# Third layer's cells: the gather's operands are swapped, and TensorE turns the rows back before the scatter

## The chip, the cores and the metric

The kernel runs on one core of one Trainium2 chip. The metric is the time of one execution in device microseconds. The kernel before took 9364.93 us, the median of 3 runs that lie between 9363.02 and 9368.05 us.

## The reference

A graph of 12,500 nodes with 128 features each and 200,000 edges goes through four layers. Each layer ends in a sum of neighbour rows over the edges and in `x = layernorm(x + layer(x))`. The edges are sorted by destination; the sources are random.

```python
edge_index = jnp.stack([src, dst])
x = _layernorm(x + _L0_gnn_ref(x, src, dst, edge_weight, L0_gnn_W1, L0_gnn_W2))   # two weighted sums
x = _layernorm(x + _L1_gnn_ref(x, ..., src, dst, edge_type_8))                    # typed edges
x = _layernorm(x + _L2_gnn_ref(x, L2_gnn_W, L2_gnn_b, src, dst, edge_weight))     # the layer changed
x = _layernorm(x + _L3_gnn_ref(x, edge_index, ...))                               # attention
```

The change is in the third layer (`_L2_gnn_ref`). Its sum is

```python
h = logmap0(x)
h = h @ W + b
msgs = edge_w[:, None] * h[edge_src]
h = jax.ops.segment_sum(msgs, edge_dst, num_segments=N)
```

## The kernel before, in words

The sum of the third layer is made in `forward_pass` (line 1342), in two ways at once. A part of the edges goes "in order": GpSimd fetches 128 rows at a time from a table in DRAM (line 1394), VectorE builds a matrix that says which row goes to which node with which weight (line 1425), and TensorE multiplies the two (`in_order`, line 1526). The rest of the edges is sorted into cells, and no row of these is fetched on its own.

A cell belongs to a window of 256 source nodes, two source tiles of 128. There are 7 passes `q` over 49 windows, so 343 cells. A cell has 512 slots in 4 blocks of 128 (`FB = 4`). In each block the first 64 slots hold edges whose source lies in tile 0 of the window, the last 64 those with a source in tile 1. One cell takes these steps:

1. SyncE loads the rows of the window from `xparts` (line 1369): each row is split into three bf16 parts whose sum is the fp32 row. It also loads from `srow` (line 1373) the list that says for each slot which source row it wants, to all partitions.
2. VectorE compares the list with the partition number (`to_slots`, line 1409): `reached[r]` is a matrix of zeros and ones, 128 source rows by 512 slots.
3. TensorE gathers (`gather`, line 1504): for each of 4 blocks, 3 parts and 2 tiles it takes the 64 slots' columns of `reached` as the stationary operand and the 128 x 128 rows of the tile's part as the moving one. That is 24 matmuls; the result stands in a PSUM bank with the slots on partitions, 64 of them from each of the two tiles.
4. ScalarE copies the bank to `had[r]` in SBUF as fp32 (`rows_out`, line 1479).
5. VectorE builds `to_dst[r]` (`to_nodes`, line 1417), 4 times 128 slots by 256 nodes, with the edges' weights.
6. TensorE scatters (`scatter`, line 1516): 4 fp32 matmuls with `had` stationary and `to_dst` moving, added into two PSUM banks. The profile shows each fp32 matmul as two records.

TensorE's stream is written out in the order `gather(u + 2)`, `scatter(u)`, and after four of seven cells one `in_order`. So it works two cells ahead. Four sets of buffers `r` go around (line 1353; the cells of a body of seven use the sets 0, 1, 2, 3, 0, 1, 2). Semaphores tie the engines: `xin` and `din` tell of the loads, `reach` of `to_slots`, `gat` of a gather done, `got` of a copy by ScalarE done, `picked` of `to_nodes`, `scat` of a scatter done. A load for a set waits for the gather that last used it (line 1368).

After each pass `q` VectorE adds the two banks to the sums (line 1459), and TensorE clears them (line 1532).

The second layer's `typed_pass` (line 1628) has a gather of its own (line 1822): there the rows' tile is stationary and the slots move, in 6 matmuls.

Of the kernel before, what the change touches and what calls it, by code (L numbers as in the profile page):

```python
# [13 lines left out]
P = 128  # L14
N = 12500
E = 200000
D = 128
# [79 lines left out]
def gnn_kernel(nc, x, src, dst, edge_type_8, edge_weight, W1, W2, Vb, w_comp, root, bias1,  # L97
# [3 lines left out]
    with ctx:  # L101
# [124 lines left out]
        for name in ("load", "copied", "made", "fin", "dve", "pe", "act", "pool", "issued",  # L226
                     "slot", "staged", "g0", "g1", "g2", "g3", "g4", "g5", "g6", "selected", "added",
                     "h1", "h1r", "proj", "projused", "tstored0", "tstored1",
                     "xin0", "xin1", "summed", "rowsT", "var", "sdev", "normed", "stored0", "kept0", "kept1",
                     "xTready", "xTfree", "saved", "tA", "tB",  # L230
                     "onehot", "prod", "packed", "resid", "inrank", "slotted", "weighed", "ranked", "counts", "cntb", "tbuilt",
                     "tsaved", "fcode", "parts", "hi", "rest", "mid", "gat", "scat", "reach", "picked",
                     "got", "sent", "based", "mixed", "scaled", "typed", "rooted", "rootkept", "closed", "natsum", "din0", "din1", "xin2", "xin3", "din2", "din3",
                     "winread", "winT", "targets", "fac", "rowcopy", "selT", "selTc", "atedge", "logit",
                     "ex", "msg", "summedE", "newrow", "newT", "wback",
                     "below", "selb", "vstage", "vT", "bstage", "runmax", "runT", "runlast", "nodemax", "mg"):
            sem(name)
# [1064 lines left out]
        run_base_i = idx[0:1, :, :].rearrange("p a k -> p (a k)")  # L1302

# [38 lines left out]
        def forward_pass(table):  # L1342
# [8 lines left out]
            rowsP = [psum[:, 4 + r, 0:FB * P] for r in range(4)]  # L1351
# [11 lines left out]
            with nc.Block() as block:  # L1363
# [104 lines left out]
                def _(act):  # L1468
# [4 lines left out]

                    def rows_out(q, it, u):
                        n = q * AW + it * FU + u
                        r, before = buffer(u)
                        act.wait_ge(sem("gat"), n + 4)
                        act.wait_ge(sem("scat"), n + (4 - before))
                        nc.scalar.activation(had[r], rowsP[r], ACT.Copy).then_inc(sem("got"), 1)

                    for j in range(3):
                        stage(j, j)
                    rows_out(0, 0, 0)
                    with act.Fori(0, FG) as q:
                        with act.Fori(0, FT7) as it:
                            for u in range(FU):
                                if u in FA:
                                    j = FA.index(u)
                                    stage(q * (FT7 * FM) + it * FM + (j + 3), (j + 3) % FM)
                                rows_out(q, it, u + 1)  # L1490

                @block.tensor
                def _(pe):
                    def gather(q, it, u):
# [4 lines left out]
                        pe.wait_ge(sem("got"), n + (4 - before))  # L1499
                        for i in range(FB):  # L1500
                            for p in range(3):
                                for t in range(2):
                                    at = i * P + t * HS
                                    last = nc.tensor.matmul(rowsP[r][t * HS:(t + 1) * HS, i * P:(i + 1) * P],  # L1504
                                                            reached[r][:, at:at + HS],
                                                            srcwin_x[r][:, t, p, :],
                                                            start=(p == 0), stop=(p == 2))
                        last.then_inc(sem("gat"), 1)
# [34 lines left out]
                    for u in range(2):  # L1543
                        gather(0, 0, u)
                    with pe.Fori(0, FG) as q:
                        pe.wait_ge(sem("sent"), q + 1)
                        clear(True)
                        with pe.Fori(0, FT7) as it:
                            for u in range(FU):
                                gather(q, it, u + 2)  # L1550
                                scatter(q, it, u)
# [1514 lines left out]
```

## Time and profile before

| | |
|---|---|
| median of 3 runs | 9364.93 us |
| span of the profiled execution | 12999.9 us |
| TensorE (PE) busy | 9231.9 us |
| mean granted TensorE clock | 0.787 |
| third layer's `forward_pass`, by its first and last gather | 8120 to 9734 us of the span |

The profile gives of the profiled execution its span alone; no time of its own stands beside it. The span is 3635 us longer than the median of the runs, so the profiled execution is much slower than the timed ones, and a duration in it is not a share of the 9364.93 us. Times of the trace count from the start of the span. PE is TensorE's matmuls, PEld its weight loads, which run beside them. In a timeline row several like instructions are merged: the first number is the start of the first, the second the busy time. The time that a group takes on TensorE is read from the start of its row to the start of the next.

### The profile page before, as it was taken

Reading aid. Unit: us, or ns where it says so; the run is one execution under the profiler, and the core shown is the slowest. Engines: PE = TensorE matmul, PEld = TensorE weight load, DVE = VectorE, ACT = ScalarE, POOL = GpSimd, SP = SyncE. Lnnn points to the kernel's source line nnn. Section 1 sums busy time; section 2 is a strip of 40 time slices with the busy share of each in tenths; the row PEclk is TensorE's granted clock in tenths of the full one; section 3 lists DMA queues with packets and bytes.
Section 4 is the critical chain, followed back from the end, with each engine's and each line's share of the span. In section 5 each row is a group of like instructions: output and inputs, shape, how many; then the busy total and the mean of one; then the engine's idle time right before and its main releaser. Section 6 shows DMA issues by size and latency. Waiting matters only on the chain. (4 is left out here: it accounts for less than half of the span.)

```text
span 12999.9 us, 294862 instructions
## 1 busy us (share of the span) xinstructions
PE 9231.9 (71%) x88712; PEld 7531.3 (58%) x88762; DVE 6869.4 (53%) x25269; ACT 3183.5 (24%) x9441; POOL 5674.7 (44%) x5790
## 2 busy tenths in 40 slices
PE   5977777777777777677777774888873555555555
PEld 5866667776766667634454453666662444444443
DVE  8964444444444444456666665555544555555555
ACT  5841111112111111241111123111113233222223
POOL 3534444442444444305555551444442555555552
PEclk8888888888888888789999996888886555555555
DMA  1013333333333333462222223333332111111113
GB/s 50 28 47 90 91 89 89 88 90 105 90 89 90 89 88 90 95 217 69 67 67 66 67 70 110 101 104 102 101 94 70 39 39 39 39 39 39 39 39 61
DMA packets 962709, 999.47 MB, mean 77 GB/s; under 512 B 141701, under 2 KB 861933, under 8 KB 962093
## 3 DMA queue, kind: packets, MB, share of 16 engines
q1 hardware_dynamic: 774502, 616.47, 17.1%
q0 software_dynamic: 174720, 364.70, 12.9%
q10 hardware_dynamic: 13255, 16.19, 0.4%
q14 instruction: 206, 1.69, 0.0%
q8 instruction: 26, 0.43, 0.0%
HBM read 858.52 MB, written 144.69 MB: 77 GB/s over the span
## 5 line engine op out<-in xcount | busy, mean ns | idle before, releaser
L497 POOL DMA_INDIRECT ring<-att_table,idx x1592 | 1556.3, 978 | 1307.7 <-ACT idx L484 715.5
L1225 PE MATMUL psum<-ring 128*128 128x128 bf16 x21276 | 1547.8, 226 | 784.6 <-issue 766.3
L1225 PEld LDWEIGHTS psum<-ring 128*128 128x128 bf16 x21276 | 1281.3, 101 | 984.9 <-issue 927.9
L1162 DVE TENSOR_SCALAR ring<-sel,iota_col 128x640 bf16<-128x640 bf16 (+1 forms) x1576 | 487.0, 369 | 2368.2 <-remote 1627.6
L1240 PE MATMUL psum<-state 64*128 64x128 f32 x14112 | 1479.8, 356 | 208.9 <-issue 206.7
L1240 PEld LDWEIGHTS psum<-state 64*128 64x128 f32 x14112 | 1318.1, 261 | 345.7 <-issue 330.0
L1148 POOL DMA_INDIRECT ring<-gcn_table,idx x980 | 932.3, 951 | 1300.6 <-ACT idx L1197 996.0
L1679 POOL DMA_INDIRECT state<-rel_table,state x1120 | 1071.1, 956 | 981.8 <-ACT state L1779 657.6
L1148 POOL DMA_INDIRECT ring<-rows,idx x980 | 933.7, 953 | 1289.0 <-ACT idx L1197 993.2
L1169 DVE TENSOR_SCALAR state<-iota_row,state 128x128 f32<-128x128 f32 x5488 | 1457.2, 356 | 0.0
L1394 POOL DMA_INDIRECT state<-hyp_table,state x784 | 755.8, 964 | 855.3 <-ACT state L1471 650.6
L1832 PE MATMUL psum<-weights,state 128*128 128x512 f32 x1576 | 911.5, 663 | 256.2 <-DVE state L1715 192.1
L1209 ACT ACTIVATE state<-psum 128x640 f32<-128x640 f32 (+1 forms) x784 | 476.8, 649 | 2390.3 <-remote 1600.9
L1715 DVE SCALAR_TENSOR_TENSOR state<-psum,state 128x128 f32<-128x128 f32 x2364 | 683.0, 345 | 450.3 <-issue 211.9
L1240 PE MATMUL psum<-state,ring 64*128 64x128 f32 x7840 | 762.1, 319 | 14.6 <-issue 14.5
L1516 PE MATMUL psum<-state 128*128 128x256 f32 x2744 | 767.9, 428 | 0.0
L2939 PE MATMUL psum<-tout 128*128 128x16 bf16 x4728 | 190.3, 173 | 747.2 <-DVE tout L2764 571.8
L1240 PEld LDWEIGHTS psum<-state,ring 64*128 64x128 f32 x7840 | 708.5, 239 | 18.3 <-issue 18.0
L2939 PEld LDWEIGHTS psum<-tout 128*128 128x128 bf16 x4728 | 156.4, 102 | 822.3 <-issue 487.1
L1516 PEld LDWEIGHTS psum<-state 128*128 128x128 f32 x2744 | 547.9, 210 | 108.8 <-issue 8.0
L1504 PE MATMUL psum<-ring,state 128*64 128x128 bf16 x8280 | 397.2, 230 | 272.4 <-issue 270.8
L1840 PEld LDWEIGHTS psum<-state 128*128 128x128 f32 x1568 | 325.1, 207 | 429.4 <-issue 416.4
(447 smaller groups left out, 15814.7 us busy)
## 6 DMA issues: line engine op xcount, KB each, us to landing
ring<-xparts SPq DMA_DIRECT2D x1332, 192.0 KB
ring<-srow SPq DMA_DIRECT2D x544, 128.0 KB
sel<-drow SPq DMA_DIRECT2D x394, 160.0 KB
sel<-drow SPq DMA_DIRECT2D x394, 128.0 KB
rel_table<-tout SPq DMA_DIRECT2D x98, 512.0 KB, 2.6
ring<-att_table,idx POOLq DMA_INDIRECT x1592
ring<-rows SPq DMA_DIRECT2D x56, 448.0 KB
xparts<-state SPq DMA_DIRECT2D x28, 672.0 KB, 3.6
```

What stands on the lines that cost most here:

```text
L497: pool.indirect_dma_start(out=ring[:, u, k, 0:width], out_offset=None, in_=table, in_offset=bass.IndirectOffsetOnAxis(ap=idx[:, u, k:k + 1 ...
L1148: pool.indirect_dma_start(out=fetched[u][:, q, :], out_offset=None, in_=table, in_offset=bass.IndirectOffsetOnAxis(ap=idx[:, u, q:q + 1], ...
L1162: ins = nc.vector.tensor_scalar(reach[u % 2][:, t, :], wanted[u], at[:, :], None, ALU.is_equal)
L1169: ins = nc.vector.tensor_scalar(picks[u][:, j, :], iota_row[:, :], tabS[:, bass.ds(n * SJ + j, 1)], tabW[:, bass.ds(n * SJ + j, 1)], ALU.i ...
L1209: nc.scalar.activation(got[u + v], rowsP[v], ACT.Copy).then_inc(sem("got"), 1)
L1225: last = nc.tensor.matmul(rowsP[v][:, j * P:(j + 1) * P], reach[v][:, t, j * P:(j + 1) * P], xwin[u][:, t, i, :], start=(t + i == 0), stop ...
L1240: last = nc.tensor.matmul(sums[h][:, j * P:(j + 1) * P], rows[h * HS:(h + 1) * HS, :], picks[u][h * HS:(h + 1) * HS, j, :], start=False, s ...
L1394: pool.indirect_dma_start(out=nat_rows[j][:, k, :], out_offset=None, in_=table, in_offset=bass.IndirectOffsetOnAxis(ap=nat_idx[j][:, k:k + ...
L1516: last = nc.tensor.matmul(sums[:, i * SW:(i + 1) * SW], had[r][:, i * P:(i + 1) * P], to_dst[r][:, i, :], start=False, stop=False)
L1679: pool.indirect_dma_start(out=type_rows[j % RB][:, k, :], out_offset=None, in_=table, in_offset=bass.IndirectOffsetOnAxis(ap=type_idx[j % ...
L1715: ins = nc.vector.scalar_tensor_tensor(out=to[:, i, :], in0=by_basis[i][:, b * D:(b + 1) * D], scalar=typeW[b][:, bass.ds(n * FB + i, 1)], ...
L1832: nc.tensor.matmul(by_basis[i], rows_T[R3[u % FU]][:, i * P:(i + 1) * P], V_all, start=True, stop=True).then_inc(sem("proj"), 1)
```

## The change

The gather is turned. The stationary operand is now a tile's part of the rows (source nodes by features), and the slots move, 256 of them at a time: 4 blocks of 64, with a stride of 128. Tile and part give 6 matmuls in place of 24. The result stands with the features on partitions. ScalarE copies it to a new buffer `asked_T[r]` (`turned_out`), TensorE turns each of the 4 blocks with a transpose against the identity back into the same bank (`turn_back`), and ScalarE copies the bank to `had[r]` as before (`rows_out`). The scatter and all other steps are as they were. Two semaphores are new: `turned` and `back`.

```diff
--- before.py
+++ after.py
@@ -231,7 +231,7 @@
...
-                     "winread", "winT", "targets", "fac", "rowcopy", "selT", "selTc", "atedge", "logit",
+                     "turned", "back", "winread", "winT", "targets", "fac", "rowcopy", "selT", "selTc", "atedge", "logit",
...
@@ -1300,6 +1300,8 @@
         nat_sel = [sel_flat[:, i * FK * WIN:(i + 1) * FK * WIN].rearrange("p (k j) -> p k j", j=WIN)
                    for i in range(FM)]
         run_base_i = idx[0:1, :, :].rearrange("p a k -> p (a k)")
+        at = 12 * D + 4 * FB * P // 2
+        asked_T = [ring_flat[:, at + w * FB * P:at + (w + 1) * FB * P] for w in range(3)] + [sq[:, 0:FB * P]]
 
         def forward_setup():
 
@@ -1348,7 +1350,11 @@
             forward_setup()
             sums = psum[:, 0:2, :].rearrange("p b c -> p (b c)")
             nat_bank = [psum[:, 2 + v, 0:WIN] for v in range(2)]
-            rowsP = [psum[:, 4 + r, 0:FB * P] for r in range(4)]
+            bank = [psum[:, 4 + r, 0:FB * P] for r in range(4)]
+
+            def halves(tile, t):
+
+                return tile.rearrange("p (i t s) -> p i t s", t=2, s=HS)[:, :, t, :]
 
             def buffer(u):
 
@@ -1471,15 +1477,23 @@
                         nc.scalar.activation(nat_idx[j], srcT[:, bass.ds(n * FK, FK)], ACT.Copy
                                              ).then_inc(sem("staged"), 1)
 
+                    def turned_out(q, it, u):
+                        n = q * AW + it * FU + u
+                        r, _ = buffer(u)
+                        act.wait_ge(sem("gat"), n + 4)
+                        nc.scalar.activation(asked_T[r], bank[r], ACT.Copy).then_inc(sem("turned"), 1)
+
                     def rows_out(q, it, u):
                         n = q * AW + it * FU + u
                         r, before = buffer(u)
-                        act.wait_ge(sem("gat"), n + 4)
+                        act.wait_ge(sem("back"), n + 1)
                         act.wait_ge(sem("scat"), n + (4 - before))
-                        nc.scalar.activation(had[r], rowsP[r], ACT.Copy).then_inc(sem("got"), 1)
+                        nc.scalar.activation(had[r], bank[r], ACT.Copy).then_inc(sem("got"), 1)
 
                     for j in range(3):
                         stage(j, j)
+                    turned_out(0, 0, 0)
+                    turned_out(0, 0, 1)
                     rows_out(0, 0, 0)
                     with act.Fori(0, FG) as q:
                         with act.Fori(0, FT7) as it:
@@ -1487,6 +1501,7 @@
                                 if u in FA:
                                     j = FA.index(u)
                                     stage(q * (FT7 * FM) + it * FM + (j + 3), (j + 3) % FM)
+                                turned_out(q, it, u + 2)
                                 rows_out(q, it, u + 1)
 
                 @block.tensor
@@ -1497,15 +1512,20 @@
                         pe.wait_ge(sem("reach"), n + 4)
                         pe.wait_ge(sem(f"xin{r}"), loaded(q, it, u))
                         pe.wait_ge(sem("got"), n + (4 - before))
+                        for t in range(2):
+                            for p in range(3):
+                                last = nc.tensor.matmul(halves(bank[r], t), srcwin_x[r][:, t, p, :],
+                                                        halves(reached[r], t), start=(p == 0), stop=(p == 2))
+                        last.then_inc(sem("gat"), 1)
+
+                    def turn_back(q, it, u):
+                        n = q * AW + it * FU + u
+                        r, _ = buffer(u)
+                        pe.wait_ge(sem("turned"), n + 1)
                         for i in range(FB):
-                            for p in range(3):
-                                for t in range(2):
-                                    at = i * P + t * HS
-                                    last = nc.tensor.matmul(rowsP[r][t * HS:(t + 1) * HS, i * P:(i + 1) * P],
-                                                            reached[r][:, at:at + HS],
-                                                            srcwin_x[r][:, t, p, :],
-                                                            start=(p == 0), stop=(p == 2))
-                        last.then_inc(sem("gat"), 1)
+                            last = nc.tensor.transpose(bank[r][:, i * P:(i + 1) * P],
+                                                       asked_T[r][:, i * P:(i + 1) * P], ident[:, :])
+                        last.then_inc(sem("back"), 1)
 
                     def scatter(q, it, u):
                         n = q * AW + it * FU + u
@@ -1542,12 +1562,14 @@
                                      start=True, stop=True).then_inc(sem("natsum"), 1)
                     for u in range(2):
                         gather(0, 0, u)
+                    turn_back(0, 0, 0)
                     with pe.Fori(0, FG) as q:
                         pe.wait_ge(sem("sent"), q + 1)
                         clear(True)
                         with pe.Fori(0, FT7) as it:
                             for u in range(FU):
                                 gather(q, it, u + 2)
+                                turn_back(q, it, u + 1)
                                 scatter(q, it, u)
                                 if u in FA:
                                     j = FA.index(u)
```

TensorE's queue, in the body of the loop over `it`, from the gather of one cell to the in-order matmuls: lines 1504, 1516 and 1526 are `gather`, `scatter` and `in_order`. Before, of the gather of cell 3 and the scatter of cell 1:

```order
L1498 ISA [waits reach]
L1504 MATMUL psum<-ring,state 64x128 [waits got,xin3]
L1504 MATMUL psum<-ring,state 64x128 x23
L1513 REGISTER_ALU
L1514 REGISTER_ALU [waits got]
L1516 MATMUL psum<-state 128x256 [waits picked]
L1516 MATMUL psum<-state 128x256 x3
```

Now (1517 is the gather, 1526 the turning back, 1536 the scatter):

```order
L1513 ISA [waits reach]
L1517 MATMUL psum<-state,ring 128x4x64 [waits got,xin3]
L1517 MATMUL psum<-state,ring 128x4x64 x5
L1526 MATMUL psum<-ident,ring 128x128 [waits turned]
L1526 MATMUL psum<-ident,ring 128x128 x3
L1533 REGISTER_ALU
L1536 MATMUL psum<-state 128x256 [waits picked,got]
L1536 MATMUL psum<-state 128x256 x3
```

Between the gather of a cell and the scatter of the cell two before it stands the turning back of the cell between, with a wait for `turned`. The scatter's 4 matmuls have the same place behind it.

ScalarE's queue in the same body: 1471 is `stage` (the indices for GpSimd), 1479 is `rows_out`. Before:

```order
L1477 REGISTER_ALU
L1478 REGISTER_ALU [waits gat]
L1479 ACTIVATE state<-psum 128x512 [waits scat]
L1477 REGISTER_ALU
L1479 ACTIVATE state<-psum 128x512 [waits scat,gat]
L1470 REGISTER_ALU
L1471 ISA [waits natsum]
L1471 ACTIVATE state<-srcT 128x4
```

Now (1477 is `stage`, 1484 is `turned_out`, 1491 is `rows_out`):

```order
L1483 REGISTER_ALU
L1484 ACTIVATE sq<-psum 128x512 [waits gat]
L1489 REGISTER_ALU
L1491 ACTIVATE state<-psum 128x512 [waits scat,back]
L1483 REGISTER_ALU
L1484 ACTIVATE ring<-psum 128x512 [waits gat]
L1489 REGISTER_ALU
L1491 ACTIVATE state<-psum 128x512 [waits scat,back]
L1476 REGISTER_ALU
L1477 ISA [waits natsum]
L1477 ACTIVATE state<-srcT 128x4
```

Each cell has two copies of 512 columns in place of one. The first waits for the gather of the cell that stands two ahead, the second for the turning back.

## Rows read from the trace of the kernel before

**Rows 1.** The page: span, TensorE's busy time, its granted clock in 40 slices.
```profile
span 12999.9 us, 294862 instructions
PE 9231.9 (71%) x88712; PEld 7531.3 (58%) x88762; DVE 6869.4 (53%) x25269; ACT 3183.5 (24%) x9441; POOL 5674.7 (44%) x5790
...
PEclk8888888888888888789999996888886555555555
```

**Rows 2.** Groups of instructions, 8120 to 9740 us (count, busy us, mean ns, idle before):
```profile
L1394 POOL DMA_INDIRECT state<-hyp_table,state x782 | 753.9, 964 | 841.3 <-ACT state L1471 636.9 <-issue 204.4
L1516 PEld LDWEIGHTS psum<-state 128*128 128x128 f32 x2744 | 547.9, 210 | 108.8 <-issue 8.0 <-ACT state L1479 0.7
L1417 DVE TENSOR_SCALAR state<-tout,state 128x256 f32<-128x256 f32 x1372 | 479.2, 413 | 0.9 <-issue 0.6
...
L1504 PEld LDWEIGHTS psum<-ring,state 128*64 128x64 bf16 x8280 | 286.1, 114 | 404.1 <-issue 375.0 <-DVE state L1409 4.8
...
L1425 DVE TENSOR_SCALAR sel<-iota_row,dstrel,wT 128x128 f32<-128x128 f32 x784 | 221.2, 353 | 0.3 <-issue 0.3
...
L1479 ACT ACTIVATE state<-psum 128x512 f32<-128x512 f32 x344 | 202.5, 597 | 803.3 <-remote 662.1 <-PE psum L1504 118.8 <-issue 21.6
L1409 DVE TENSOR_SCALAR state<-ring,iota_col 128x512 bf16<-128x512 bf16 x345 | 124.0, 359 | 656.4 <-DMA ring<-srow 623.4 <-issue 28.4 <-PE psum L1504 3.5
```

**Rows 3.** Timeline of TensorE in the third layer (start us, busy us):
```profile
8602.44 0.86 PE L1504 MATMUL psum<-ring,state 128*64 128x128 bf16 x24
8603.24 1.99 PE L1516 MATMUL psum<-state 128*128 128x256 f32 x8
8605.16 0.86 PE L1504 MATMUL psum<-ring,state 128*64 128x128 bf16 x24
8605.95 1.99 PE L1516 MATMUL psum<-state 128*128 128x256 f32 x8
8607.78 1.05 PE L1526 MATMUL psum<-sel,state 128*128 128x128 f32 x8
8608.76 0.41 PE L1504 MATMUL psum<-ring,state 128*64 128x128 bf16 x8
```

**Rows 4.** The same timeline, where single matmuls stand apart:
```profile
8563.58 0.23 PE L1504 MATMUL psum<-ring,state 128*64 128x128 bf16 x1 [0.45 <-issue]
8565.00 0.23 PE L1504 MATMUL psum<-ring,state 128*64 128x128 bf16 x1 [1.18 <-issue]
8565.72 0.22 PE L1504 MATMUL psum<-ring,state 128*64 128x128 bf16 x1 [0.50 <-issue]
...
8567.85 0.76 PE L1504 MATMUL psum<-ring,state 128*64 128x128 bf16 x20 [0.50 <-issue]
```

**Rows 5.** Timeline of TensorE in the second layer's typed pass:
```profile
6209.02 0.82 PE L1822 MATMUL psum<-ring 128*128 128x256 bf16 x6
6209.67 1.02 PE L1832 MATMUL psum<-weights,state 128*128 128x512 f32 x2
6210.53 0.59 PE L1840 MATMUL psum<-state 128*128 128x256 f32 x2
6210.97 1.02 PE L1832 MATMUL psum<-weights,state 128*128 128x512 f32 x2
...
6212.26 1.05 PE L1852 MATMUL psum<-sel,state 128*128 128x128 f32 x8
6213.15 0.59 PE L1832 MATMUL psum<-weights,state 128*128 128x512 f32 x1
```

**Rows 6.** Timeline of TensorE, seven fp32 transposes in the projection:
```profile
5573.84 0.93 PE L2264 MATMUL psum<-ident,ring 128*128 128x128 f32 x7
```

**Rows 7.** Timeline of TensorE, seven fp32 transposes ahead of the third layer:
```profile
7899.64 1.76 PE L2105 MATMUL psum<-ident,ring 128*128 128x128 f32 x7 [2.55 <-ACT ring L2068]
```

**Rows 8.** Timeline of ScalarE beside rows 3, the copy after the first gather:
```profile
8603.42 0.60 ACT L1479 ACTIVATE state<-psum 128x512 f32<-128x512 f32 x1 [0.56 <-PE psum L1504]
```

**Rows 9.** Busy us and count of each engine, granted clock, DMA share in one stretch:
```profile
8500.00:9000.00 500.00, 408.01 (x3929) 329.65 (x3934) 257.80 (x851) 72.52 (x169) 235.69 (x244) 0.88 0.37 103
```

## The prediction

> **What bounds the kernel now.** I read the page first. TensorE is busy for 9231.9 of the span's 12999.9 us [rows 1]. The timed runs take 9364.93 us, 3635 us less than the span, and TensorE idles in the span for 12999.9 - 9231.9 = 3768 us. So nearly all of TensorE's idle time in the profile would have to be missing from the timed runs. That decides how the rest is read: what TensorE has to stream is real, what it stands still for in this profile mostly is not. One reservation: the mean granted clock is 0.787, and matmuls that ran at the lower level would be shorter in a run with fewer stops, so a part of the idle time could survive.
>
> Next the groups of the third layer's cells, 8120 to 9740 us, some 1615 us between first and last gather, for 343 cells: 4.7 us a cell. The reader is to see which engine lacks slack [rows 2]. ScalarE is busy for 202.5 us with its copies, VectorE for 479.2 + 221.2 + 124.0 us with its large groups. GpSimd is a different matter: its rows are 0.96 us each, and 4 of them serve one in-order step. TensorE has the most to do. Its weight loads for the gather waited 375.0 us for nothing that the profile shows, 4.8 us for VectorE and, before the scatter, 0.7 us for ScalarE. VectorE waited 623.4 us for the lists from DRAM, but TensorE nearly never waited for VectorE, so these loads arrive early enough.
>
> The 375.0 us have a shape [rows 4]: single matmuls of one gather start 0.7 or 1.4 us apart, and then 20 run at full rate. A gather outside such a stop takes the same time again and again. The timeline without stops gives the floor of TensorE [rows 3], from start to start:
> - gather 8605.95 - 8605.16 = 0.79 us
> - scatter 8605.16 - 8603.24 = 1.92 us if a gather follows, 8607.78 - 8605.95 = 1.83 us if the in-order step follows
> - in-order step 8608.76 - 8607.78 = 0.98 us
>
> A body of seven cells with four in-order steps takes 3 x (0.79 + 1.92) + 4 x (0.79 + 1.83 + 0.98) = 22.5 us, 3.22 us a cell, 1104 us for 49 bodies. The granted clock was 0.88 in 500 us of this stage, stops included [rows 9]; the rows of the floor are at its upper level, 2.4 GHz. GpSimd needs 16 x 0.964 + 204.4 / 49 = 19.6 us in a body, fetches and the "issue" gaps between them [rows 2]: near, but shorter than 22.5. VectorE's three groups are (479.2 + 221.2 + 124.0) / 49 = 16.8 us. I take it that in the timed runs TensorE bounds this stage.
>
> **The gather.** 24 matmuls with 64 stationary columns go, 6 with 128 stationary and 256 moving columns come. The trace has this form, in the second layer [rows 5]: 6209.67 - 6209.02 = 0.65 us for six, in the same strided reading of the slots. Against 0.79 us that is -0.14 us a cell.
>
> The old form costs its neighbours too. The same 8 in-order records take 6213.15 - 6212.26 = 0.89 us in the second layer, and 0.98 us before the gather of 64 columns. The scatter is 1.92 us before that gather and 1.83 before another step. So -0.09 us a cell where TensorE enters the form. The 8 records of the scatter should take less still: two records of that shape take 6210.97 - 6210.53 = 0.44 us in the second layer, and two of twice the width 6210.53 - 6209.67 = 0.86 us, so 8 take 1.72 to 1.76 us and not 1.83. I take 1.73. I read the missing 0.10 us as the first weight load, which the narrow gather ahead of it holds up. This is the least certain gain. Together -0.33 us a cell with it, -0.23 without.
>
> A rule speaks against this. The Trainium skill, TensorEngine Tiling (Array Packing), section Theoretical Speedup, gives two matmuls with at most 64 stationary columns up to twice the throughput, as they run side by side in halves of the array. By it 24 matmuls of 128 moving columns stream as long as 12, and 12 x 128 is 6 x 256: the turn would gain nothing in the gather. The section Key Properties adds that a change of tiling mode drains the engine. The trace bears out both: 0.79 against 0.65 us is a small gain for a quarter of the matmuls, and the 0.09 us at the border look like the drain. By the first rule alone the sum below would be 343 x 0.44 = 151 us.
>
> **The turning back.** 4 fp32 transposes of 128 x 128 come to each cell. Seven of them took 0.93 us with a last one of 0.27 us [rows 6], so (0.93 - 0.27) / 6 = 0.11 us each: +0.44 us. At the lower clock seven took 1.76 us [rows 7], 0.22 us each. I take 0.11, since the neighbours here are dense.
>
> **Sum.** New cell: 0.65 + 0.44 + 1.73 = 2.82 us, with the in-order step 3.71. Old: 2.71 and 3.60 (2.72 and 3.61 as the trace repeats them). That is +0.11 us a cell, 343 x 0.11 = +38 us. Bounds: without the gain at the scatter +0.21 us, +72 us; with transposes that stream as the pairs of the old gather do, 0.79 / 12 = 0.07 us each, -0.05 us a cell, -17 us; with all transposes at the lower clock, +0.55 us, +189 us. I take +40 us, from the rows at the upper clock, and 9364.93 + 40 = 9405 us. In the profile's own terms the span would go to 13,040 us if the stops stayed.
>
> **What is hidden.** ScalarE's added copy is 0.60 us [rows 8], 343 x 0.60 = 206 us of work on an engine with 1.2 us of 3.3 us used. It costs nothing while it comes in time. After a gather ends (8603.30) the copy starts at 8603.42. So `turned` of cell n + 2 is there some 0.7 us after its gather, and TensorE asks for it one step later, 3 us on. Behind `turned_out` of n + 2 on ScalarE stands `rows_out` of n + 1, which also waits for the turning back of n + 1. It starts at about 0.65 + 0.12 + 0.60 = 1.4 us after the gather began, ends at 2.0, and the scatter of n + 1 asks for it at 2.8 + 1.1 = 3.9 us. Slack 1.9 us. The bank of a set is free one step later than before, and its next gather comes a step after that. `stage` now stands behind a later copy, by up to 2 us, and each fetch is ordered a whole body ahead. The loads wait for `gat` as before; SyncE's and GpSimd's queues keep their order. If the cover were gone, the wait would be one copy a cell, 206 us.
>
> **Rivals.**
> 1. Faster: the stops are real, at least in part. They stand at the gathers of narrow matmuls [rows 4] and the code that causes them shrinks: a body has 7 x 64 + 64 = 512 matmul and load records before and 7 x 36 + 64 = 316 after, 38% fewer. If the 375.0 us were in the timed runs and scaled with the count, 0.38 x 375 = 143 us would go: 9365 + 40 - 143 = 9262 us; with half of the stops 9333 us. It decides from the point where more than 105 us of the 375 (40 / 0.38) exist in a timed run. For it: the stops are always at L1504 here. Against: 3635 us must be missing from the profile's time.
> 2. No change: loads or GpSimd pace the stage at 3.3 us a cell or more, and the added work fills TensorE's waits: 9365 to 9380 us. For it: VectorE's 623.4 us of waiting for lists. Against: the 4.8 us of TensorE.
> 3. Slower: ScalarE's chain ends last. A wait of 0.3 us a cell adds 103 us: 9508 us. Against: the slack of 1.9 us.
> 4. Slower: TensorE falls to its lower level more often, since the transposes carry less load. If the clock fell in one cell of ten, 0.1 x 343 x 3.4 = 117 us: 9522 us. For it: rows 7. Against: rows 6 are at the upper level without a dense neighbour.
>
> The Trainium skill, TensorE: Matmul & The Clock Gate, section Part 4: PE-mode transpose, has it that transposes do not count as work for the clock gate. It would make rival 4 likelier; rows 6 neither prove nor refute it, since other work ran before.
>
> **How the numbers follow.** What a measurement of this kernel can tell from no change is about 0.2%, 19 us. Forecast (+19 to +80 us): 0.56. Rivals 3 and 4, or any cost over +80: 0.10. Between -19 and +19: 0.16, rival 2 and the low bound of the sum. Rival 1: 0.18. So faster 0.18, same 0.16, slower 0.66. The range leaves out a half of rival 1 and most of rivals 3 and 4: 9330 to 9465 us. The likeliest case's own range is 9384 to 9445.
>
> **What would show it.** Six gather matmuls start to start in 0.65 us; four transposes in 0.44 us; eight scatter records in 1.73 us (1.83 would put +72 in place of +38); the in-order step in 0.89 us. No wait of TensorE for ScalarE at the turning back or the scatter above a few us. A granted clock of 0.85 or more in the stage. The forecast is wrong if a body without stops is shorter than 22.5 us, if TensorE's stops shrink and the timed runs follow, or if a body is bound at GpSimd's 19.6 us.

## The result and the profile after

| | before | after |
|---|---|---|
| median of 5 runs | 9364.93 us | 9400.06 us |
| lowest, highest | 9363.02, 9375.23 us | 9390.7, 9409.83 us |
| ratio, 95% interval | | 1.0036, [1.0023, 1.0048] |
| predicted | | 9405 us (9330 to 9465) |

The changed kernel is slower by 35 us, between 22 and 45 us by the interval. Forecast were 40 us.

The page of the changed kernel, with span and busy time:

```profile
span 9388.9 us, 285834 instructions
PE 7707.4 (82%) x83928; PEld 6594.8 (70%) x83928; DVE 6867.2 (73%) x25269; ACT 3450.3 (37%) x9786; POOL 5726.0 (61%) x5790
```

Its span is 9388.9 us, as long as a timed run. The span of [rows 1] was 12999.9 us. The two profiles can't be compared stage by stage before it is known what made the first one long; the first experiment is about that.

TensorE's timeline in the third layer's cells (start us, busy us; 1517 is the gather, 1526 the turning back, 1536 the scatter, 1546 the in-order step):

```profile
6204.44 0.82 PE L1517 MATMUL psum<-state,ring 128*128 128x256 bf16 x6
6205.10 0.60 PE L1526 MATMUL psum<-ident,ring 128*128 128x128 f32 x4
6205.53 1.89 PE L1536 MATMUL psum<-state 128*128 128x256 f32 x8
6207.26 1.05 PE L1546 MATMUL psum<-sel,state 128*128 128x128 f32 x8
6208.15 0.82 PE L1517 MATMUL psum<-state,ring 128*128 128x256 bf16 x6
```

From start to start: gather 0.66 us, turning back 0.43, scatter 1.73, in-order step 0.89. These rows answer to [rows 3], where a gather took 0.79, a scatter 1.83 to 1.92 and the in-order step 0.98 us. A cell with an in-order step is 6208.15 - 6204.44 = 3.71 us.

Busy us, count, granted clock, DMA share and GB/s of 500 us of the stage, which answers to [rows 9]:

```profile
5800.00:6300.00 500.00, 482.33 (x3218) 433.08 (x3217) 342.96 (x1129) 164.42 (x366) 309.85 (x326) 0.98 0.51 135
```

TensorE is busy for 482.33 of 500 us at a granted clock of 0.98, so nearly all of this stretch runs at the upper of the two levels, 2.4 GHz, although four transposes stand in each cell. GpSimd's 309.85 us and VectorE's 342.96 us leave both slack.

Groups of the stage (count, busy us, mean ns, idle before), which answer to [rows 2]:

```profile
L1517 PEld LDWEIGHTS psum<-state,ring 128*128 128x128 bf16 x2070 | 204.6, 99 | 54.4 <-issue 9.5 <-DVE state L1415 4.1
L1491 ACT ACTIVATE state<-psum 128x512 f32<-128x512 f32 x344 | 203.5, 592 | 1.8 <-PE psum L1526 1.8
```

TensorE's weight loads for the gather waited 9.5 us for nothing that shows and 4.1 us for VectorE. No line of the whole list has TensorE waiting for ScalarE. ScalarE's copies of one cell in the timeline (1484 is `turned_out`, 1491 `rows_out`):

```profile
6205.30 0.60 ACT L1484 ACTIVATE ring<-psum 128x512 f32<-128x512 f32 x1 [1.64 <-PE psum L1517]
...
6205.79 0.59 ACT L1491 ACTIVATE state<-psum 128x512 f32<-128x512 f32 x1
```

They follow each other without a gap. The second ends at 6205.79 + 0.59 = 6206.38, 1.94 us after the gather began, and the scatter that wants it begins one step later, after 6208.15.

### The profile page after: what moved, and what is told of

Same layout as the page of the kernel before. It is cut to its first block and busy times, and to the rows that moved or that the text cites. A ratio compares the mean times of both kernels' runs of the same rounds, so it can differ in the third digit from the quotient of the medians.

```text
span 9388.9 us, 285834 instructions
## 1 busy us (share of the span) xinstructions
PE 7707.4 (82%) x83928; PEld 6594.8 (70%) x83928; DVE 6867.2 (73%) x25269; ACT 3450.3 (37%) x9786; POOL 5726.0 (61%) x5790
## 5 line engine op out<-in xcount | busy, mean ns | idle before, releaser
L1225 PE MATMUL psum<-ring 128*128 128x128 bf16 x21276 | 1271.4, 221 | 54.6 <-DVE ring L1162 54.6
L1240 PE MATMUL psum<-state 64*128 64x128 f32 x14112 | 958.7, 278 | 0.0
L1240 PEld LDWEIGHTS psum<-state 64*128 64x128 f32 x14112 | 850.7, 188 | 44.4 <-issue 4.8
L1854 PE MATMUL psum<-weights,state 128*128 128x512 f32 x1576 | 815.2, 599 | 42.8 <-DVE state L1737 42.8
L1536 PE MATMUL psum<-state 128*128 128x256 f32 x2744 | 652.8, 381 | 0.0
L1815 ACT ACTIVATE state<-psum,state 128x128 f32<-128x128 f32 x788 | 289.9, 368 | 810.5 <-PE psum L1854 809.7
L1240 PE MATMUL psum<-state,ring 64*128 64x128 f32 x7840 | 568.7, 272 | 0.0
L1197 ACT ACTIVATE idx<-state 128x3 int32 (+2 forms) x788 | 160.7, 204 | 1032.8 <-PE psum L1240 923.8
L1240 PEld LDWEIGHTS psum<-state,ring 64*128 64x128 f32 x7840 | 502.8, 188 | 0.0
L1423 DVE TENSOR_SCALAR state<-tout,state 128x256 f32<-128x256 f32 x1372 | 474.8, 407 | 0.0
```

The source lines that it names most:

```text
L1225: last = nc.tensor.matmul(rowsP[v][:, j * P:(j + 1) * P], reach[v][:, t, j * P:(j + 1) * P], xwin[u][:, t, i, :], start=(t + i == 0), stop ...
L1240: last = nc.tensor.matmul(sums[h][:, j * P:(j + 1) * P], rows[h * HS:(h + 1) * HS, :], picks[u][h * HS:(h + 1) * HS, j, :], start=False, s ...
L1536: last = nc.tensor.matmul(sums[:, i * SW:(i + 1) * SW], had[r][:, i * P:(i + 1) * P], to_dst[r][:, i, :], start=False, stop=False)
L1854: nc.tensor.matmul(by_basis[i], rows_T[R3[u % FU]][:, i * P:(i + 1) * P], V_all, start=True, stop=True).then_inc(sem("proj"), 1)
```

## The experiments

Theory A is the prediction's: TensorE's stream bounds the stage, and each change counts by its start-to-start times. All times are medians; the kernels ran in three batches, and each batch ran the kernel before as well (9353.72, 9359.21 and 9358.05 us). A difference is against the kernel before of the same batch.

### The kernel before, profiled again

No edit.

> The kernel before, unchanged, profiled once more. Theory A (TensorE's stream bounds the stage, and the stops of the first profile are not part of a timed run): the span comes near 9365 us, the third layer's cells take about 1165 us, a body of seven 22.5 us, and the gather's "issue" idle time falls from 375 us to under 20. Theory B (the stops belong to the narrow matmuls): the stage takes about 1615 us again, with a stop in nearly every body.

Measured: one run of 9343.64 us. Its page, the weight loads of its gather in the stage, and TensorE's timeline:

```profile
span 9341.8 us, 294912 instructions
PE 7739.6 (83%) x88762; PEld 6557.2 (70%) x88762; DVE 6851.6 (73%) x25269; ACT 3293.7 (35%) x9441; POOL 5716.6 (61%) x5790
```

```profile
L1504 PEld LDWEIGHTS psum<-ring,state 128*64 128x64 bf16 x8280 | 246.7, 111 | 85.9 <-issue 57.9 <-DVE state L1409 4.2 <-ACT state L1479 0.8
```

```profile
6202.11 0.86 PE L1504 MATMUL psum<-ring,state 128*64 128x128 bf16 x24
6202.90 1.99 PE L1516 MATMUL psum<-state 128*128 128x256 f32 x8
6204.73 1.05 PE L1526 MATMUL psum<-sel,state 128*128 128x128 f32 x8
6205.72 0.86 PE L1504 MATMUL psum<-ring,state 128*64 128x128 bf16 x24
```

The span is 9341.8 us. The "issue" idle time before the gather's weight loads, 375.0 us in [rows 2], is 57.9 us, more than the 20 us I expected; the full-width gather of the changed kernel has 9.5, so most of it seems to come with the entry into the narrow form. No matmul stands apart as in [rows 4]. The durations are those of [rows 3]: 0.79, 1.83 and 0.99 us. So the stops belonged to that one profiled execution, and Theory B falls. They did not belong to narrow matmuls even there: the first layer's gather (line 1225), whose matmuls have 128 stationary columns, was stretched as well, from 2735 us in the new profile to 4592 us in the first, with 1694.3 us of "issue" idle time in 2444 places against 42.7 us in 13. The new row comes first:

```profile
L1225 PE MATMUL psum<-ring x21276: 219/219/314, 868.1 to 3603.4; 128*128 128x128 bf16 x199
```

```profile
L1225 PE MATMUL psum<-ring x21276: 216/219/314, 873.8 to 5465.9; 128*128 128x128 bf16 x199
```

In 500 us of the third layer's stage the kernel before has the granted clock of the changed one, 0.98, where [rows 9] had 0.88 with the stops:

```profile
5800.00:6300.00 500.00, 482.45 (x5350) 405.24 (x5349) 348.59 (x1165) 102.62 (x228) 319.99 (x335) 0.98 0.52 139
```

With this profile the stage can be compared; the rows give times of single records and the start of the first and last scatter, of the kernel before and of the changed one:

```profile
L1516 PE MATMUL psum<-state x2744: 379/379/796, 5735.0 to 6896.7; 128*128 128x256 f32 x196
```

```profile
L1536 PE MATMUL psum<-state x2744: 379/379/635, 5735.2 to 6930.0; 128*128 128x256 f32 x196
```

6896.7 - 5735.0 = 1161.7 us against 6930.0 - 5735.2 = 1194.8 us: +33 us, nearly the whole of the 35 us. The two spans differ by 47 us; the other 14 us lie behind the stage, where the kernels are alike, and are not the change's.

### The turned gather without the turning back

```diff
-                        act.wait_ge(sem("back"), n + 1)
+                        act.wait_ge(sem("gat"), n + 4)
...
-                                turned_out(q, it, u + 2)
...
-                                turn_back(q, it, u + 1)
```

> The turned gather alone: ScalarE's added copy and the four transposes are left out, so the scatter gets rows that are not turned back. Theory A: per cell 0.65 + 1.73 us in place of 0.79 + 1.92, and 0.89 in place of 0.98 for the in-order step: -0.33 us x 343 = -113 us against before, 9252 us. Theory C (array packing alone: 12 x 128 columns are 6 x 256, nothing is gained): no change, 9365 us. Theory D (the stage is paced by loads or GpSimd): no change either, but with waits of TensorE in the profile.

Measured: 9236.52 us, ratio 0.9873 [0.9856, 0.9889] to before, which is -117 us against 9353.72. Theory A said -113. TensorE's timeline (1514 gather, 1533 scatter, 1543 in-order step):

```profile
6208.62 0.82 PE L1514 MATMUL psum<-state,ring 128*128 128x256 bf16 x6
6209.27 1.89 PE L1533 MATMUL psum<-state 128*128 128x256 f32 x8
6211.00 1.05 PE L1543 MATMUL psum<-sel,state 128*128 128x128 f32 x8
6211.89 0.82 PE L1514 MATMUL psum<-state,ring 128*128 128x256 bf16 x6
```

The gather takes 0.65 us, the scatter 1.73 and the in-order step 0.89. Theories C and D said no change: both fall for this kernel. The turned gather alone is a real gain.

### The old gather with the turning back

In the changed kernel:

```diff
-                        for t in range(2):
+                        for i in range(FB):
                             for p in range(3):
-                                last = nc.tensor.matmul(halves(bank[r], t), srcwin_x[r][:, t, p, :],
-                                                        halves(reached[r], t), start=(p == 0), stop=(p == 2))
+                                for t in range(2):
+                                    at = i * P + t * HS
+                                    last = nc.tensor.matmul(bank[r][t * HS:(t + 1) * HS, i * P:(i + 1) * P],
+                                                            reached[r][:, at:at + HS],
+                                                            srcwin_x[r][:, t, p, :],
+                                                            start=(p == 0), stop=(p == 2))
```

> The old gather of 24 narrow matmuls, with ScalarE's added copy and the four transposes behind it, so the scatter gets the rows turned once too often. Theory A: the transposes cost 4 x 0.11 = 0.44 us a cell, but they also stand between the narrow gather and the scatter and take over its late first weight load, so +0.40 to +0.44 us: +137 to +150 us against before, 9502 to 9515 us. Theory D (paced elsewhere): under +60 us.

Measured: 9491.7 us, ratio 1.0149 [1.0132, 1.0166], +138 us. TensorE's timeline (1519 gather, 1530 turning back, 1540 scatter):

```profile
6204.27 0.66 PE L1530 MATMUL psum<-ident,sq 128*128 128x128 f32 x4
6204.77 1.89 PE L1540 MATMUL psum<-state 128*128 128x256 f32 x8
6206.59 0.86 PE L1519 MATMUL psum<-ring,state 128*64 128x128 bf16 x24
```

The scatter takes 1.82 us before a gather, where it took 1.92 in [rows 3]: the late first weight load has gone to the transposes, which take 6204.77 - 6204.27 = 0.50 us here and 0.43 in the changed kernel (medians over the stage 0.49 and 0.44). So the narrow gather does delay what stands behind it, whatever that is; that it does so through the first weight load is read from the start times and not shown apart. Per cell 0.50 - 0.10 = 0.40 us, 137 us by 343 cells, and 138 are measured. The two halves give -117 + 138 = +21 us, and together they are +35. The late load explains the rest: the first half saves all its 0.10 us, the second turns it into 0.06 us at the transposes and saves 0.04 us, but the change can save it only once. 0.04 x 343 = 14 us have to be added to the 21. This is read from the rows; each of the two ratios is uncertain by some 16 us, so the times alone do not show these 14 us.

### ScalarE's added copy alone

The old gather stands in the changed kernel, as in the section before; `turn_back` is left out, and `rows_out` waits for `turned` in place of `back`. So ScalarE copies each bank twice, and nobody reads the first copy.

> The kernel before with ScalarE's added copy of each bank and without transposes: `rows_out` copies the bank a second time, behind a copy that nobody reads. Theory A (the added copy is hidden): no change, within 10 us of before. Theory F (a part of the change's +0.4% is ScalarE's second copy): slower by the same share, up to 0.60 us x 343 = 206 us if it lay open.

Measured: 9360.37 us, ratio 1.0 [0.9991, 1.0009]. 343 copies of 0.60 us on ScalarE cost nothing that can be measured (8 us at most by the interval). Theory F falls.

### One part of the rows in place of three

```diff
-                            for p in range(3):
+                            for p in range(1):
...
```

> The kernel before with one of the three bf16 parts of the rows gathered and two left out: 8 narrow matmuls a cell in place of 24. Theory A (fixed cost of 0.28 us a cell at the borders of the narrow form, plus 0.056 us for each pair): 8 pairs fewer, -0.45 us x 343 = -154 us, and in the profile the in-order step stays 0.98 us, the scatter 1.92 and 1.83 us. Theory G (the border cost is a tail of the 24 matmuls and shrinks with them): those three shrink too, up to -0.28 us x 2/3 x 343 = -64 us more, -218 us. Where TensorE comes below 19.6 us a body GpSimd could take over: TensorE's body would be 22.6 - 3.1 = 19.5 us, so a part of the 154 us may not come.

Measured: 9211.83 us, ratio 0.9844 [0.983, 0.9857], -147 us. TensorE's timeline:

```profile
6204.87 1.05 PE L1526 MATMUL psum<-sel,state 128*128 128x128 f32 x8
6205.85 0.41 PE L1504 MATMUL psum<-ring,state 128*64 128x128 bf16 x8
6206.20 2.00 PE L1516 MATMUL psum<-state 128*128 128x256 f32 x8
6208.12 0.41 PE L1504 MATMUL psum<-ring,state 128*64 128x128 bf16 x8
```

The in-order step before the gather is 6205.85 - 6204.87 = 0.98 us and the scatter before a gather 6208.12 - 6206.20 = 1.92 us, as with 24 matmuls. The gather is 0.35 us. Over all cells the medians are 0.791 and 0.344 us, so the 8 pairs that go took 0.056 us each; 4 pairs are 0.224 us, and 0.12 us of the gather is fixed. Theory G falls: the cost at the borders is the same for 8 and for 24 matmuls. It is 0.12 + 0.09 + 0.10 us a cell, 0.316 before rounding, a little more than the 0.28 that I had put down.

### The turning back without cover

```diff
-                                turn_back(q, it, u + 1)
+                                turn_back(q, it, u + 2)
```

(and in the prologue the turning back behind each of the two gathers)

> The changed kernel with the turning back directly behind the gather of the same cell, so that nothing covers ScalarE's first copy. Theory A: TensorE waits for the gather's tail, the copy of 0.60 us and the signals, about 0.95 us a cell less the little that stays hidden: 343 x 0.85 to 0.95 = +290 to +325 us against the changed kernel, near 9700 us. Rival: the 64-deep queue of work behind it hides a part and it is under +150 us.

Measured: 9721.52 us, ratio 1.0388 [1.0374, 1.0402] to before: +362 us, and +321 against the changed kernel's 9400. TensorE's timeline:

```profile
6205.90 0.82 PE L1517 MATMUL psum<-state,ring 128*128 128x256 bf16 x6
6207.41 0.66 PE L1526 MATMUL psum<-ident,ring 128*128 128x128 f32 x4 [0.69 <-ACT ring L1484]
6207.90 1.89 PE L1536 MATMUL psum<-state 128*128 128x256 f32 x8
```

The turning back now starts 1.51 us after the gather in place of 0.66: +0.85 us, and its own time is 0.49 in place of 0.43 us, 0.91 x 343 = 312 us. This is what the order of the changed kernel, one cell between gather and turning back, is worth. The transposes' 0.49 us are those of the run with the old gather, though no narrow gather stands here: a start behind a wait costs them the same.

### Fewer borders: gathers in groups

If the borders of the narrow form cost 0.3 us a cell, the kernel before can shed them without any turning. In its body on TensorE, with groups of four and three:

```diff
-                            for u in range(FU):
-                                gather(q, it, u + 2)
-                                scatter(q, it, u)
-                                if u in FA:
+                            for group in ((0, 1, 2, 3), (4, 5, 6)):
+                                for u in group:
+                                    gather(q, it, u + 2)
+                                for u in group:
+                                    scatter(q, it, u)
+                                    if u in FA:
...
```

> The kernel before with another order on TensorE: in each body of seven cells the gathers stand in two groups, four and three, with their scatters and in-order steps behind them. Same matmuls. Theory A (each entry into the narrow form costs 0.09 us and each exit 0.19 us): 5 of 7 entries and exits go, 5 x 0.28 x 49 = 69 us, 9296 us. Theory E (the old gather is dear in itself and its borders cost nothing): no change. If the tighter order makes TensorE wait for VectorE or ScalarE at a group's start, slower.

Measured: 9488.98 us, ratio 1.0141 [1.0124, 1.0158], +135 us where I had expected -69. TensorE's timeline and VectorE's over the same time (1409 `to_slots`, 1417 `to_nodes`, 1435 `add_before`):

```profile
6201.38 0.86 PE L1504 MATMUL psum<-ring,state 128*64 128x128 bf16 x24 [1.88 <-DVE state L1409]
6203.34 0.86 PE L1504 MATMUL psum<-ring,state 128*64 128x128 bf16 x24 [1.10 <-DVE state L1409]
```

```profile
6200.57 0.27 DVE L1435 TENSOR_TENSOR acc<-acc,psum 128x128 f32 x1
6200.77 0.34 DVE L1409 TENSOR_SCALAR state<-ring,iota_col 128x512 bf16<-128x512 bf16 x1
6201.03 1.38 DVE L1417 TENSOR_SCALAR state<-tout,state 128x256 f32<-128x256 f32 x4
6202.83 0.39 DVE L1409 TENSOR_SCALAR state<-ring,iota_col 128x512 bf16<-128x512 bf16 x1 [0.41 <-DMA ring<-srow]
...
6208.89 0.29 DVE L1435 TENSOR_TENSOR acc<-acc,psum 128x128 f32 x1 [3.25 <-PE psum L1526]
```

The gathers at 6201.38 and 6203.34 each start 0.5 to 0.6 us after the VectorE comparison at 6200.77 and 6202.83. The first of these comparisons stands in VectorE's queue behind `to_nodes` of a cell and behind `add_before`, and the `add_before` at 6208.89 waited 3.25 us for an in-order step on TensorE, which now stands later. The second, for the fourth gather of the group, waited for its list from DRAM. In the kernel text the load for a cell waits for the gather three cells before it (line 1368 waits for `gat` at `n + 1`, and `gat` starts at 3), and of a fourth cell that is the first gather of its own group. So TensorE's order had been changed without that of its partners, VectorE and SyncE.

> The kernel before with TensorE's gathers in groups of two, two, two and one, and nothing else moved. The groups of four failed because VectorE's comparison for the third and fourth gather stood behind its waits for in-order steps. Theory A: with pairs each comparison is ready, 3 of 7 entries and exits of the narrow form go, 3 x 0.28 x 49 = -41 us against before. Theory H (any group makes TensorE wait for VectorE): no change or slower, with waits at L1504 for L1409.

The edit is the same with groups of two, two, two and one. Measured: 9313.23 us, ratio 0.9948 [0.9935, 0.9962], -46 us, where -41 were expected. TensorE's timeline:

```profile
6202.11 1.53 PE L1504 MATMUL psum<-ring,state 128*64 128x128 bf16 x48
6203.57 3.72 PE L1516 MATMUL psum<-state 128*128 128x256 f32 x16
6207.13 1.05 PE L1526 MATMUL psum<-sel,state 128*128 128x128 f32 x8
6208.11 1.53 PE L1504 MATMUL psum<-ring,state 128*64 128x128 bf16 x48
```

Two gathers take 6203.57 - 6202.11 = 1.46 us, not 1.58, and the two scatters behind them 6207.13 - 6203.57 = 3.56 us, not 1.92 + 1.83 = 3.75. None of these gathers waits. The first and last scatter of the stage:

```profile
L1516 PE MATMUL psum<-state x2744: 379/379/796, 5750.1 to 6864.5; 128*128 128x256 f32 x196
```

6864.5 - 5750.1 = 1114.4 us against 1161.7: -47 us, and 3 borders x 0.316 us x 49 bodies are 46. Theory H falls.

> The changed kernel with its turned gathers in groups of two, two, two and one, as the kernel before had them in the run that was 46 us faster. Theory A (the borders that grouping takes away are those of the narrow form, 0.12 + 0.09 + 0.10 us each): the turned gather has no such border, so no change against the changed kernel, 9395 to 9405 us. Theory I (grouping helps by itself, through fewer waits or a steadier stream): 30 us or more faster than the changed kernel.

The same pairs in the changed kernel, with each turning back ahead of its scatter. Measured: 9399.7 us, ratio 1.0045 [1.0032, 1.0059] to before, +42 us where the changed kernel had +35, its own time within the intervals. So pairs save nothing where no narrow gather stands: what they save in the kernel before is the narrow form's border. Theory I falls.

> The kernel before with TensorE's gathers in groups of three, two and two. Theory A: 4 of 7 borders of the narrow form go, 4 x 0.316 x 49 = -62 us against before, if VectorE's comparison for the third gather is there in time; where it is not, waits at L1504 for L1409 eat it, up to 2 us a body, 98 us.

Groups of three, two and two. Measured: 9415.2 us, ratio 1.006 [1.0046, 1.0074], +57 us. TensorE's timeline:

```profile
6218.81 1.53 PE L1504 MATMUL psum<-ring,state 128*64 128x128 bf16 x48
6222.18 0.86 PE L1504 MATMUL psum<-ring,state 128*64 128x128 bf16 x24 [1.84 <-DVE state L1409]
```

The third gather of the group of three starts 3.37 us after the first two and waits 1.84 us for VectorE. The saving of 62 us is more than eaten.

The last regrouping has groups of four and three on TensorE and the same groups on VectorE:

```diff
-                            for u in range(FU):
-                                to_slots(q, it, u + 2)
-                                to_nodes(q, it, u)
+                            for group in ((0, 1, 2, 3), (4, 5, 6)):
+                                for u in group:
+                                    to_slots(q, it, u + 2)
+                                for u in group:
+                                    to_nodes(q, it, u)
...
```

> Groups of four and three, as in the run that was 135 us slower, but with VectorE's comparisons for a group also standing together, ahead of its other work for the group. Theory A: if the waits for VectorE go, 5 of 7 borders go, 5 x 0.316 x 49 = -77 us against before. If VectorE's in-order steps still stand between the groups, the waits at the head of the second group stay, up to 2 us a body, and it is near or above before.

Measured: 9568.69 us, ratio 1.0222 [1.0208, 1.0236], +211 us. One group of four in the timeline (1373 the load of a list, 1409 `to_slots`, 1506 gather, 1518 scatter, 1528 in-order step; other rows are left out):

```profile
6198.43 2.20 PE L1506 MATMUL psum<-ring,state 128*64 128x128 bf16 x72
6200.05 0.35 SPq L1373 DMA_DIRECT2D ring<-srow  x1
6203.48 0.35 DVE L1409 TENSOR_SCALAR state<-ring,iota_col 128x512 bf16<-128x512 bf16 x1 [5.74 <-DMA ring<-srow]
6203.96 1.49 PE L1506 MATMUL psum<-ring,state 128*64 128x128 bf16 x24 [3.33 <-DVE state L1409]
6205.39 5.85 PE L1518 MATMUL psum<-state 128*128 128x256 f32 x16
6211.08 1.05 PE L1528 MATMUL psum<-sel,state 128*128 128x128 f32 x8
```

Three gathers run without a wait. The list for the fourth is ordered only at 6200.05, after the first of them is done, and the comparison comes 3.43 us later; VectorE waited 5.74 us for it, and TensorE 3.33 us for the comparison. This is the load's wait again, which VectorE's new order does not touch. The stop has a second price: TensorE's clock falls. Busy us, count, granted clock, DMA share of the 4 us behind the stop:

```profile
6204.00:6208.00 4.00, 4.00 (x30) 3.37 (x31) 4.00 (x14) 0.00 (x0) 2.19 (x3) 0.50 0.67 199
```

At a granted clock of 0.50, the lower level, the fourth gather takes 1.43 us in place of 0.79, and the two scatters 5.69 us in place of 3.56. From 5800 to 6300 us the granted clock is 0.88 here, 0.96 in the runs with groups of four on TensorE alone and of three, and 0.98 in those with pairs and without groups. TensorE's waits for the comparison are much the same with VectorE's old order and its new one (158 and 164 us), so it is in the clock that the last 76 us, from +135 to +211, were for the most part lost: the two scatters between gathers and in-order step alone take 54 us more in all, 8 us of it in waits for `to_nodes`. An earlier load of the lists and another order of `add_before` were not tried. Pairs are the best version that makes the whole sum, 46 us below before and 87 us below the changed kernel's 9400.

## Why the prediction was right

**What bounds the stage.** That the stops are not in a timed run was the point on which all rested, and the second profile of the kernel before bears it out: 9341.8 us, gathers without stops. Rival 1, the stops, had 0.18 and is refuted. But the step that led there was in part luck. It set the 3768 us in which TensorE was idle beside the 3635 us of difference, as if nearly all idle time had to go. In the second profile TensorE is still idle for 9341.8 - 7739.6 = 1602 us, and its busy time is 1492 us shorter; the prediction's reservation about the lower clock points that way, but it puts no size to it. That the two numbers stood so close was chance. [rows 3], gathers at the upper clock without stops, were the sound part of the argument. That GpSimd's 19.6 us a body does not bind holds at 22.6 and at 23.3 us. In the run with one part TensorE's body is 19.4 us by its start-to-start times, and 7 of the expected 154 us were missing. GpSimd was not seen to take them: of the cells' matmuls the gather waited 8.5 us and the scatter 3.1 us for VectorE (7.0 and none in the kernel before), and the in-order step, which uses GpSimd's rows, for nothing.

**The gather.** -0.14 us by the second layer's rows; measured 0.79 to 0.66. The second layer's kernel text has the same form, and its duration carried over.

**The neighbours.** -0.09 at the entry and -0.10 at the scatter: measured 0.98 to 0.89, and 1.83 to 1.73. The second was "the least certain gain", and it decided between +38 and +72 us. The run with the old gather and the turning back shows it apart from the rest, and the single-part run shows that it does not shrink with the number of matmuls. How the hardware makes it is inferred from start times alone.

**The packed matmuls.** By the Trainium skill, TensorEngine Tiling (Array Packing), section Theoretical Speedup, alone the turn would gain nothing and the sum would be +151 us. The streams agree with it (12 narrow pairs at 0.056 us against 6 matmuls at 0.11). The Trainium skill has in the section Key Properties of that page that a change of tiling mode drains the engine; the runs agree, with a cost of 0.32 us a cell that does not depend on the number of matmuls, but none shows that a drain makes it. The gain of the turned gather is the border that it avoids, not its stream: 12 x 0.056 = 0.67 us is about the turned gather's time.

**The turning back.** 4 x 0.11 us; measured 0.43. Rival 4 did not come about: the granted clock is 0.98 in 500 us of the stage, with four transposes in each cell and without them. The Trainium skill, TensorE: Matmul & The Clock Gate, section Part 4: PE-mode transpose, has it that transposes do not count as work for the clock gate; here that made no difference, and what a stage of transposes alone would do, no run here shows.

**ScalarE.** Hidden, as forecast. Rival 3 is refuted by the copy alone (ratio 1.0) and by the changed kernel's own groups, where TensorE does not wait for ScalarE. The cover was priced by the run without it: 312 to 321 us, where I had put down one copy a cell, 206 us. That bound was too low, since the wait holds the gather's tail and the signals too: the first transpose comes 0.85 us later than behind a cover, not 0.60.

**The sum.** 2.82 us a cell and 3.71 with the in-order step, measured and forecast alike; +38 us in the sum, +33 in the profiles, +35 in the times.

## What to carry to other kernels

When a profiled span is far above the timed runs, take the profile once more if that can be had. If not, price changes from start-to-start times in stretches without stops; an agreement of the idle time with the missing time proves little, since a low clock lengthens the busy time too. A matmul form costs at its borders as well: before swapping operands to leave a narrow form, and paying for transposes, see whether the narrow matmuls can stand together. When the order on one engine is changed, follow each buffer that the others prepare for it, back to the load: the regroupings gave -46, +57, +135 and +211 us, and a wait that is long enough to bring the clock down is paid twice.

## What the runs showed of the hardware

- The same program gave a profile of 12999.9 us with stops of 0.7 and 1.4 us between single matmuls, and one of 9341.8 us without them; both do the same work. In the first the stops stood in the first layer's gather of 128 stationary columns as well. What made them is open.
- A group of matmuls with 64 stationary columns costs 0.32 us besides its stream, by its borders: 0.09 us before it, 0.12 within it and 0.10 in the fp32 matmuls behind it (0.06 where transposes follow), the same for 8 and 24 matmuls. Two such groups side by side pay it once.
- fp32 transposes of 128 x 128 follow each other every 0.11 us at the upper clock, and four of them in each cell left the granted clock at 0.98.
- In the run with groups of four on both engines TensorE waited 3.33 us in a body and then had a granted clock of 0.50 for 4 us, where 16 fp32 records took 5.69 us in place of 3.56.
